# A two-layer graph and expert network: first layer's lists in four column groups of TensorE, the routing's tile multiply on ScalarE

## The reference, cut to what matters

```python
# layer 0, experts: each of 16 experts chooses its k = 468 rows (k = 3750 // 16 * 2)
logits = jnp.einsum('bsd,de->bse', x, gate_weight)
affinity = jax.nn.softmax(logits, axis=-1).transpose(0, 2, 1)
gating, index = jax.lax.top_k(affinity, k)
x_in = jnp.take_along_axis(x[:, None, :, :], index[..., None], axis=2)
h = jax.nn.gelu(jnp.einsum('bekd,edh->bekh', x_in, w1) + b1[None, :, None, :])
x_e = jnp.einsum('bekh,ehd->bekd', h, w2) + b2[None, :, None, :]
out = out.at[jnp.arange(Bx)[:, None], idx_flat].add(weighted)   # weighted = gating * x_e
# layer 1, experts: each row chooses its two best of 8 experts
routing = jax.nn.softmax(xf @ Wr.T + br, axis=-1)
sel_w, sel_idx = jax.lax.top_k(routing, 2)
```

## Time and profile before

| | |
|---|---|
| median of 3 runs | 3113.9 us (3112.03 to 3117.18) |
| the profiled execution | 3120.04 us, its span 3118.3 us |
| PE busy | 2675.0 us (86%) |
| DVE busy | 1871.9 us (60%) |
| POOL busy | 1623.8 us (52%) |
| ACT busy | 727.3 us (23%) |
| granted TensorE clock, mean | 0.938 of full speed |

### The profile page before, as it was taken

One profiled execution on the slowest core, in us unless ns is written; L12 is line 12 of the kernel. 1 busy time (PEld: TensorE's weight loads), 2 busy tenths in 40 slices (PEclk: granted clock), 3 DMA queues, 4 the chain that ended last, 5 costly groups with the idle time before them and its releaser, 6 DMA issues. The chain is left out here.

```text
span 3118.3 us, 40184 instructions
## 1 busy us (share of the span) xinstructions
PE 2675.0 (86%) x10312; PEld 1261.7 (40%) x10313; DVE 1871.9 (60%) x3301; ACT 727.3 (23%) x1355; POOL 1623.8 (52%) x1517
## 2 busy tenths in 40 slices
PE   6899799899987981999999698898988989656998
PEld 4444332222223541555554344433223223244776
DVE  6785876666666867533231456697666666675343
ACT  2002310111111771121111110032111111253665
POOL 4674277777772000344443047507777777613665
PEclk8999899999998985899999799999999999867999
DMA  7483277777774431365565449437777777575776
GB/s 268 113 137 107 79 211 211 211 211 210 211 210 146 143 118 61 92 153 146 139 152 125 158 145 174 99 140 204 211 210 211 211 211 210 153 251 135 134 135 111
DMA packets 341635, 511.11 MB, mean 164 GB/s; under 512 B 174570, under 2 KB 179930, under 8 KB 340966
## 3 DMA queue, kind: packets, MB, share of 16 engines
q0 software_dynamic: 115872, 317.04, 40.2%
q1 hardware_dynamic: 95462, 183.58, 17.2%
q10 hardware_dynamic: 130144, 8.52, 2.8%
HBM read 422.33 MB, written 86.65 MB: 163 GB/s over the span
## 5 line engine op out<-in xcount | busy, mean ns | idle before, releaser
L1226 POOL DMA_INDIRECT zg<-z_rows,src_groups x940 | 898.0, 955 | 480.4 <-issue 273.2
L1305 PE MATMUL bank<-zg,aggregate_onehot 128*128 x1888 | 941.6, 625 | 105.5 <-DVE zg L1273 98.0
L1273 DVE TENSOR_TENSOR zg<-zg,bank 128x1024 f32<-128x1024 f32 x470 | 573.4, 1220 | 409.8 <-DMA zg<-z_rows,src_groups 409.6
L1305 PEld LDWEIGHTS bank<-zg,aggregate_onehot 128*128 128x128 f32 x1888 | 305.4, 189 | 740.0 <-issue 726.8
L828 PE MATMUL bank<-alpha,front_table 128*64 128x512 bf16 x2304 | 268.5, 388 | 20.1 <-DVE alpha L681 20.1
L355 PE MATMUL bank<-zg,x 128*128 128x512 f32 x480 | 219.3, 613 | 11.8 <-PEq L371 11.2
L2185 PE MATMUL bank<-exp_w,exp_h_t 128*117 128x512 f32 x512 | 225.8, 595 | 0.7 <-ACT exp_h_t L2132 0.7
L2039 POOL DMA_INDIRECT x_rows<-exp_y,exp_add_tok x64 | 137.0, 2141 | 159.1 <-DVE exp_y L2092 146.3
L2177 PE MATMUL bank<-exp_xg_t,exp_w 128*128 128x468 f32 x512 | 205.8, 561 | 0.7 <-ACT exp_xg_t L2121 0.7
L828 PEld LDWEIGHTS bank<-alpha,front_table 128*64 128x64 bf16 x2304 | 133.4, 112 | 152.4 <-issue 51.6
L1251 DVE TENSOR_TENSOR aggregate_onehot<-bank,columns 128x256 f32<-128x256 f32 x472 | 192.0, 416 | 0.0
(11 more groups left out here) (453 smaller groups left out, 3342.2 us busy)
## 6 DMA issues: line engine op xcount, KB each, us to landing
exp_w<-in_L_ffn_w SPq DMA_DIRECT2D x32, 1024.0 KB, 7.6
zg<-src_key SPq DMA_DIRECT2D x48, 512.0 KB, 4.9
zg<-z_rows,src_groups POOLq DMA_INDIRECT x940, 3.7
zg<-src_tile SPq DMA_DIRECT2D x96, 128.0 KB, 3.4
exp_w<-in_L_ffn_W SPq DMA_DIRECT2D x2, 4096.0 KB, 15.8
x_rows<-zg SPq DMA_DIRECT2D x10, 768.0 KB, 3.5
hn_rows<-zg SPq DMA_DIRECT2D x10, 768.0 KB, 4.0
x<-x_rows SPq DMA_DIRECT2D x5, 1536.0 KB, 14.5
```

Of the source, the lines that this page charges most:

```text
L1226: pool.indirect_dma_start(zg[:, r, j, :], None, k.z_rows[:, :], bass.IndirectOffsetOnAxis(k.src_groups[:, n:n + 1], 0)).then_inc(gathered[ ...
L1273: v.tensor_tensor(z, z, bcast_last(scales[:, at:at + J * H], DH), ALU.mult).then_inc(msg_ready, 1)
L1305: mm = nc.tensor.matmul(k.banks[:, bass.ds(bank, 1), :].rearrange("p a n -> p (a n)"), onehot_at(n)[:, j, :], zg[:, bass.ds(at, 1), j, :]. ...
```

## The change

It has five parts.

1. `sum_list`: operands swapped. The values (20, or 32 with the neighbour's, wide) are now the weights and the 117 one-hot columns are streamed. Tile t goes to column group t % 4 of TensorE, so four partial sums stand on partitions 0, 32, 64 and 96 of the bank. ACT copies the 128 x 117 partial sums to `parts` (`take_parts`), PE adds and transposes them with one float32 matmul against `fold` (`fold_list`), ACT copies the 117 x 20 result as before. In a round the fold comes one quarter later than the sum; the wait for the copied list moves from before the first f to before f = 1.
2. PE's rounds are written out (`for` in place of `Fori`) on PE alone.
3. The first values are those of expert 0 only; those of 1 and 2 come after `place_list(0, 0)`. `read_list(0, 0)` and its token copy now come before `place_list(1, 1)`. The first expert's gathers have a semaphore per quarter.
4. `front` of layer 1: the first block of x is loaded as two halves, and statistics of the first half wait only for that.
5. `route1`: the bias is loaded in `finish_layer1`; two steps on rows beyond the last move into the wait for the exp; the two multiply and reduce pairs become one pair of twice the width; the tile multiply moves from DVE to ACT as 30 pieces, which PE awaits by pieces; the seven steps of `te` become a compare and a reduce on one partition.

```diff
+                    if layer == 1 and b == 0:
+                        for j in range(0, SBT, X_FIRST):
+                            sp.dma_start(k.x[:, j:j + X_FIRST, :], ...).then_inc(x_first if j == 0 else x_loaded[b], 16)
+                        return
...
-                values_by_quarter(k, chain, slice(0, LISTED_FIRST))
+                values_by_quarter(k, chain, slice(0, 1))
...
                 place_list(0, 0)
+                v.tensor_reduce(fold[:, :], k.ident.rearrange("p (c s) -> p s c", c=KC)[:, 0:QF, :], AX, ALU.add).then_inc(fold_ready, 1)
+                chain(values_by_quarter(k, chain, slice(1, LISTED_FIRST)))
                 v.tensor_copy(k.ps[7][:, 0:PQ], k.iota[:, 0:PQ]).then_inc(lanes_ready, 1)
-                place_list(1, 1)
                 read_list(0, 0)
                 v.tensor_copy(gather_tok[:, 0, :], tokens[:, 0:Q0]).then_inc(gather_tok_ready, 1)
+                place_list(1, 1)
...
+                def take_parts(n, bank):
+                    act.wait_ge(list_summed, n + 1)
+                    act.wait_ge(list_copied, n)
+                    nc.scalar.copy(parts[:, :], k.ps[bank][:, 0:PQ]).then_inc(parts_copied, 1)
...
                     for t in range(NT):
-                        mm = nc.tensor.matmul(k.ps[bank][0:PQ, 0:Q0 * 5], placed[:, b, t, :],
-                                              k.by_quarter[:, bass.ds(n, 1), t, :, :].rearrange("p a q f -> p (a q f)"),
-                                              start=(t == 0), stop=(t == NT - 1))
+                        g, width = t % KC, GROUP if t < NT - 1 else QF
+                        mm = nc.tensor.matmul(k.ps[bank][g * GROUP:g * GROUP + width, 0:PQ], values_of(n, t, width), placed[:, b, t, :],
+                                              start=(t < KC), stop=(t >= NT - KC), skip_group_check=True)
                     mm.then_inc(list_summed, 1)
+                def fold_list(n, bank):
+                    pe.wait_ge(parts_copied, n + 1)
+                    nc.tensor.matmul(k.ps[bank][0:PQ, 0:QF], parts[:, :], fold[:, :], start=True, stop=True).then_inc(list_folded, 1)
...
-                        if not last:
-                            pe.wait_ge(list_copied, i * U + (u + AHEAD0))
                         for f in range(F):
+                            if f == 1 and not last:
+                                pe.wait_ge(list_copied, i * U + (u + AHEAD0))
...
+                            if q == 2 and u < lists:
+                                pe.wait_ge(xg_t_ready, i * (U * Q0) + (u * Q0 + Q0 + 2))
+                                fold_list(i * U + (u + AHEAD0), 1)
...
-                with pe.Fori(0, LISTING) as i:
+                for i in range(LISTING):
...
-                dve.wait_ge(br_loaded, 16)
...
+                dve.wait_ge(consts, 1)
+                chain(v.tensor_scalar(inv[:, :], k.valid[:, :], -1.0, 1.0, ALU.mult, ALU.add))
+                for s in range(2):
+                    v.tensor_scalar(beyond[:, :, s], inv[:, :], dump[:, s:s + 1], None, ALU.mult)
                 dve.wait_ge(from_act, 1)
...
-                for s in range(2):
-                    chain(v.tensor_tensor(tmp[:, :, :], oh[:, s, :, :], slot_e[:, :, :], ALU.mult))
-                    chain(v.tensor_reduce(slot_f[:, :, s], tmp[:, :, :], AX, ALU.add))
...
+                chain(v.tensor_tensor(tmp[:, :, :, :], oh[:, :, :, :], slot_e[:, :, :].unsqueeze(1).to_broadcast([P, 2, NT, E1]), ALU.mult))
+                chain(v.tensor_reduce(slot_f[:, :, :].rearrange("p t s -> p s t"), tmp[:, :, :, :], AX, ALU.add))
+                chain(v.tensor_tensor(slot_f[:, :, :], slot_f[:, :, :], beyond[:, :, :], ALU.add))
...
-                chain(v.tensor_scalar(named[:, :, 0, :], high, k.pid[:, 0:1], None, ALU.mult))
-                tile = k.iota_bf[:, 1:NT + 1].unsqueeze(2).unsqueeze(3).to_broadcast([P, NT, 2, MT])
-                by_tile = high.rearrange("p (t s) m -> p t s m", s=2)
-                chain(v.tensor_tensor(by_tile, by_tile, tile, ALU.mult))
-                dve.sem_inc(named_ready, 1)
+                v.tensor_scalar(named[:, :, 0, :], high, k.pid[:, 0:1], None, ALU.mult).then_inc(named_ready, 1)
...
-                for e in range(E1 - 1):
-                    chain(v.scalar_tensor_tensor(te[:, :], tile_at[:, :], ends[:, e:e + 1], te[:, :], ALU.is_ge, ALU.add))
+                chain(v.tensor_tensor(passed_ends[:, :, :], bcast_last(tile_at[0:1, :], E1 - 1), ends[0:1, 0:E1 - 1].unsqueeze(1).to_broadcast([1, MT, E1 - 1]), ALU.is_ge))
+                chain(v.tensor_reduce(te[:, :], passed_ends[:, :, :], AX, ALU.add))
...
+                act.wait_ge(named_ready, 1)
+                for t in range(NT):
+                    by_tile = named[:, 2 * t:2 * t + 2, 1, :]
+                    nc.scalar.activation(by_tile, by_tile, ACT.Copy, scale=float(t + 1)).then_inc(tile_named, 1)
...
-                pe.wait_ge(named_ready, 1)
                 for n in range(W2):
                     if n % WB == 0:
                         pe.wait_ge(low_ready, n // WB + 1)
+                        pe.wait_ge(tile_named, (n + WB + 1) // 2)
```

More of the change, by code:

```diff
@@ L491, in stats @@
                 def stats(b):
-                    dve.wait_ge(x_loaded[b], 32 if layer == 0 and b == NT // SBT - 1 else 16)
+                    if layer == 1 and b == 0:
+                        dve.wait_ge(x_first, 16)
+                    else:
+                        dve.wait_ge(x_loaded[b], 32 if layer == 0 and b == NT // SBT - 1 else 16)
                     for j in range(SBT):
+                        if layer == 1 and b == 0 and j == X_FIRST:
+                            dve.wait_ge(x_loaded[b], 16)
                         ins = v.bn_stats(bn[:, b % 2, j, :], k.x[:, b * SBT + j, :])
@@ L1989, in experts0 @@
         listed = sb("listed", [PQ, AHEAD0 + U, Q0, 5], F32)
+        QF, GROUP = Q0 * 5, 32
+        parts = sb("parts", [P, PQ], F32)
+        fold = sb("fold", [P, QF], F32)
+        values_of = lambda n, t, width: k.by_quarter[:, :, :, :, :].rearrange("p e t q f -> p (e t q f)")[:, n * (NT * QF) + t * QF:n * (NT * QF) + t * QF + width]
         part = sb("part", [PQ, 2, Q0], F32)
@@ L1993, in experts0 @@
         gathered = [sem(f"gathered{u}") for u in range(U)]
+        first_gathered = [sem(f"first_gathered{q}") for q in range(Q0)]
         gather_tok_ready, add_tok_ready, added, added_all, passed = (
             sem("gather_tok_ready"), sem("add_tok_ready"), sem("added"), sem("added_all"), sem("passed"))
[L1996 removed]
+        placed_ready, list_summed, parts_copied, list_folded, list_copied, fold_ready = (sem(n) for n in ("placed_ready", "list_summed", "parts_copied", "list_folded", "list_copied", "fold_ready"))
         ranks_taken, rest_listed, lanes_ready = sem("ranks_taken"), sem("rest_listed"), sem("lanes_ready")
@@ L2020, in _, with gather @@
             def _(pool):
-                def gather(n, u):
+                def gather(n, u, first=False):
                     wait_here(pool, gather_tok_ready, n + 1, passed)
@@ L2043, in _ @@
                 for u in range(U):
-                    gather(u, u)
+                    gather(u, u, u == 0)
                 with pool.Fori(0, ER - 1) as i:
@@ L2326, in _ @@
                 v.tensor_tensor(both[:, :, :].rearrange("p e t -> p t e"), oh[:, 0], oh[:, 1], ALU.add).then_inc(to_pe, 1)
-                v.tensor_tensor(tmp[:, :, :], oh[:, 0], bcast_last(k.weights[:, :, 0], E1), ALU.mult)
+                v.tensor_tensor(tmp[:, 0], oh[:, 0], bcast_last(k.weights[:, :, 0], E1), ALU.mult)
                 chain(v.tensor_tensor(combine[:, :, :], oh[:, 1], bcast_last(k.weights[:, :, 1], E1), ALU.mult))
-                v.tensor_tensor(combine[:, :, :], combine[:, :, :], tmp[:, :, :], ALU.add).then_inc(combine_ready, 1)
+                v.tensor_tensor(combine[:, :, :], combine[:, :, :], tmp[:, 0], ALU.add).then_inc(combine_ready, 1)
                 dve.wait_ge(from_pe, 1)
```

57 lines of the change are left out of this document (33 added, 24 removed).

## The result

The changed kernel takes 3089.8 us (median of 4 runs, 3085.8 to 3090.8) against 3115.5 (3112.0 to 3121.6) for the kernel before beside it: ratio 0.9913, 95% interval 0.9894 to 0.9931. A second set gave 3087.8 against 3118.0, 0.9899 [0.9877, 0.9922]. The gain is therefore 26 to 30 us; 18.1 were forecast, 3095.8 us with a range from 3089 to 3105. The sign was right and the mechanisms mostly were, but the size was too small. The profiled executions differ by more than the medians, 3120.0 and 3089.5 us (spans 3118.3 and 3087.8); in the second set they differ by less, spans 3114.6 and 3090.7.

A forecast was written before the change was run, and what follows sets the result against it. PE was taken to bound the rounds of `experts0`, and DVE's chain `route1`. The parts, 7.8 + 0 + 1.9 + 0 + 8.4 = 18.1 us, off the 3113.9 us median gave 3095.8 us, range 3089 to 3105.

The forecast's parts named there:

- the wave of grouped matmuls: Lists in rounds: four groups' matmuls run at once, 0.075 us a wave, eight waves 0.60 us, ends 0.48 and 0.86.
- the changes of grouping: Lists in rounds: PE's wait entering and leaving grouped matmuls, 0.10 us each, ends 0 and 0.14 each.
- the rows of all four quarters there before the third list: Start of `experts0`: gathered rows there at 1257.4, transposes start at 1257.8 bound by the third list, semaphores per quarter worth nothing.
- Part 1, forecast 7.8: 13 lists in rounds of `experts0`: each 1.12 us in place of 1.67, gain 0.6 each, 7.8 us; ends 2.0 and 12.1.
- rival A: List matmuls: the pair's 56 ns pace is fixed, a list costs 2.2 us, total gain 4.1, 3109.8 us; chance 0.08.
- Part 3, forecast 1.9: First lists of `experts0`: transposes 2.5 us earlier, less a share for the half clock; 1.9 us taken, ends 0.5 and 3.
- The half that was to be given back for the clock: First product of `experts0`: if the clock's rise from 0.50 comes no earlier, 1.2 of the 2.5 us is lost.
- Part 5, forecast 8.4: `route1`: DVE's chain shortens by 8.5 us if DVE stays last; 8.4 taken, ends 7 and 8.6.
- rival B: `route1`: ACT's bf16 writes are slow, 30 pieces take 12.6 to 15 us, gain 2 to 4.5; 3101 us; chance 0.08.
- C: Small list matmuls don't overlap, 107 ns a pair, a list costs 3.7 us; slower than before, 3129.6 us; chance 0.04.
- D: More than forecast: waves at 0.06 us and a clock that rises earlier, 22 to 25 us gained, 3090 us; chance 0.08.
- The condition that I gave: Forecast wrong if a grouped list's pair costs over 40 ns or an untouched stage moves over 3 us through the clock.

The follow-up runs named there:

- unrolled: The kernel before with only PE's 12 looped rounds written out: 3114.7 us, ratio 0.9988 [0.9975, 1.0000].
- lanes_psum: The changed kernel, but the second list's `placed` compares with lane numbers in PSUM, not SBUF: 3091.7 us, 0.9910 [0.989, 0.9929].
- in_turn: The changed kernel, but tile t goes to column group t // 8, not t % 4, eight matmuls in a row per group: 3099.7 us, 0.9949.

## Why the prediction fell short

Two steps of the working failed. In part 1 the wave of grouped matmuls and the changes of grouping were put too high, by 0.27 us a list. In part 3 the working had the rows of all four quarters there before the third list, and the semaphores per quarter worth nothing; the rows came 2 us after it, and those semaphores are what kept PE from waiting for them. The stages give 23.6 us for the whole, so the rest of the measured 26 to 30 lies in no term, and its cause is open.

**Part 1, forecast 7.8, measured 10.3** (13 x 0.79; 9.9 against the rounds of `unrolled`, 29.58). The mechanism was right, overlap of four groups, and rival A's fixed pace is half right: within a group the pair keeps its 52 to 55 ns. The term that was mis-sized is the wave, 0.075 us in the working; it is 0.052 to 0.055. The nearest row says about 0.06 for 132 columns, and the 56 ns of before's own pair was at hand; the working added a margin to the first and used the second only in rival A. The two changes of grouping, 0.10 each, are mis-sized too: eight waves are 0.43, so everything else up to the next operation is 0.10 together. Sum and changes were put at 0.80 and are 0.53. The rest, 0.92 - 0.53 = 0.39 us a round, was put at 0.32; the fold is 0.13 of it (put at 0.22), and no row divides the other 0.26.

**Part 2, forecast 0: right** but for 0.03 to 0.06 us a round.

**Part 3, forecast 1.9 for the start of `experts0`.** From the stage's start to the first product it is 2.66 us (82.51 to 79.85), and 0.4 more in the first round. The transposes start at 1257.3 on the old time scale, the 1257.8 of the forecast, and the third list's sum holds them, as said. The step that failed is the gather. The rows were to be there at 1257.4. The first gather went out at 1248.9, as worked out, but was held for 2.7 us by `placed`, and the last rows landed at 1259.2 to 1260.0 in the traces of the changed kernel. That collision was not among the things weighed, though both operations overlap by the plan of the change; without it (`lanes_psum`) they land at 1256.5, and the working would have held. With one semaphore for all four quarters the transposes could not have started before the last landing, so the first product would come some 2 us later, an estimate from these landings (77.2 to 78.0 us), the transposes' 3.4 us and the 0.7 behind them; the kernel was not run that way. So "worth nothing there" is wrong by most of the gain. The short sums are the other condition: in `in_turn`, where they are slower, the transposes start at 77.15 and the product at 81.24. DVE's new order brings 0 to 0.4 us (79.82 without it). The half that was to be given back for the clock wasn't: the clock rose 83.3 us into the stage in place of 86.8.

**Part 4, forecast 0: right** in the median. In front, L738's successor starts 10.12 us into the stage, within the 10.1 to 10.5 named.

**Part 5, forecast 8.4, measured 9.0** from DVE's first operation to its last (47.73 to 38.75 us), 9.8 in the stage with the clock. Of the 9.0, 4.5 are the tile multiply and 1.1 `te`; each term was a little low, and the sum of 8.5 had been rounded down to 8.4. ACT's piece took 0.206 us: rival B is out, and the estimate of 0.20 from the Trainium skill ("ScalarE: Activation LUTs", What ACT_TABLE_LOAD costs) agrees.

**The rivals and the range.** C is out: no pair costs 107 ns. (A's sum takes 6.2 us for 13 x 0.5; by its own list of 2.2 us it is 6.4, which moves 3109.8 by 0.2.) D, 22 to 25 us and 3090, is the one that came out, for both of its reasons: a wave under 0.06 and a clock that rises earlier. It had a chance of 0.08, although its wave was the value nearest to the row. All terms at their better ends, 12.1 + 3 + 0.5 + 8.6 = 24.2, give 3089.7, which is where the range ended. The median of 3089.8 lies just inside, by luck of the base: its own neighbours had 3115.5. The ratio, on the base of 3113.9, gives 3086.8, below the range. What lies below is not in any term: the clock gave 0.8 us more in experts1, and the jumps of single stages, over 5 us in layer 1's front, had no place in the range.

What stays open: 2 to 6 us of the measured gain, which no stage that the change touches shows. The condition that I gave, that an untouched stage moves by over 3 us through the clock, came true: layer 1's front took 238.2 and 237.5 us in the kernel before and 232.4 in `unrolled`, which leaves it alone. Layer 0's graph step moved by 3.3 to 3.5 between two executions of one kernel. That the clock does it is seen for the front alone.

## To carry to other kernels

Small matmuls that follow each other at a fixed pace gained by column groups, four in the time of one, and an order that alternates groups is worth more than one that finishes a group first. When a chain is reordered, ask which wait ends last afterwards, and check what the moved DMA issue now runs beside: here a gather on POOL waited for a DVE compare with both inputs in SBUF. A semaphore for each quarter lets PE start on the rows that have landed. Sum a prediction's better ends too, and don't read a stage's gain from one pair of executions when its granted clock differs.

## What was not expected of the hardware

- A column group's pace is the same 52 to 55 ns for 32 columns held and 117 streamed as for 117 held and 20 streamed, and with eight in a row the next group starts 230 ns in, when three of the eight are still to come: 30 matmuls in 1.12 us in turn, 0.70 in pairs, 0.53 in fours.
- An indirect gather beside a DVE compare with two SBUF inputs took 3.70 us on POOL, with one input in PSUM 1.01.
- The granted clock in one place differs between executions of kernels that are alike there: in the first round of `experts0` it cost 0 to 1.9 us, in layer 1's front the stretch at 0.50 lasted 3.4 to 10.2 us and moved the stage between 231 and 239 us. Work for PE ahead of that stretch did not remove it; in `experts1` it shortened it from 13.7 to 3.4 us.
